# A recommender tower whose loops are unrolled, with an eighth table looked up by matmul and its feature store transposed

## The reference, cut to what matters

```python
e = jnp.stack([tbl_0[ids[:, 0]], ..., tbl_25[ids[:, 25]]], axis=1)      # 2048 x 26 x 128
combined = jnp.concatenate([dense[:, None, :], e], axis=1)              # 27 features of 128
interactions = jnp.einsum('bfd,bgd->bfg', combined, combined)           # a 27 x 27 gram for each sample
flat = interactions[:, triu_i, triu_j]                                  # its 351 pairs
h = jnp.concatenate([dense, flat, dense], axis=1)                       # 607 columns
h = jnp.maximum(h @ W_top1 + b_top1, 0.0)                               # 512
h = jnp.maximum(h @ W_top2 + b_top2, 0.0)                               # 256
y = h @ W_top3                                                          # 2048 x 1
```

## Time and profile before

| | value |
|---|---|
| timed executions, median | 425.34 us |
| span of the profiled execution | 696.8 us |
| mean granted clock of TensorE in it | 0.740 |
| PE, DVE, ACT, POOL busy in it | 54%, 30%, 13%, 45% |
| share of the ending chain put down to "issue" | 29% |
| share put down to "another core or an unknown queue" | 16% |

### The profile page before, as it was taken

The page is one execution under the profiler, slowest core; times in us unless marked ns, Lnnn a source line. Parts: engine busy times, 40 slices in busy tenths (PEclk is TensorE's granted clock), DMA queues, the critical chain, the costliest instruction groups (busy, mean ns, idle before and its releaser), DMA issues.

```text
span 696.8 us, 13458 instructions
## 1 busy us (share of the span) xinstructions
PE 377.1 (54%) x5828; PEld 317.6 (46%) x5828; DVE 209.2 (30%) x561; ACT 92.9 (13%) x159; POOL 312.2 (45%) x308
## 2 busy tenths in 40 slices
PE   1306523396284843927349082771817547194897
PEld 1306422394174732717238071561716545083875
DVE  3524007140083100921029010461006600075121
ACT  1111000021011200202002020100201011011132
POOL 6770546304537054470736617174271733637100
PEclk9757755598588775977769595695858858588798
DMA  5651111111101111030101201012010200101000
GB/s 163 189 159 61 41 38 47 31 54 37 41 15 53 64 42 34 21 104 4 49 26 29 100 12 53 16 38 87 20 53 8 98 26 27 49 7 52 19 3 2
DMA packets 18087, 34.32 MB, mean 49 GB/s; under 512 B 8241, under 2 KB 10929, under 8 KB 18065
## 3 DMA queue, kind: packets, MB, share of 16 engines
q0 software_dynamic: 9728, 19.94, 10.0%
q1 hardware_dynamic: 8338, 14.06, 6.1%
HBM read 33.97 MB, written 0.01 MB: 49 GB/s over the span
## 4 chain that ended last, share of the span: by engine, by line
PE 47%; issue 29%; another core or an unknown queue 16%; DMA 4%; ACT 3%; DVE 1%; SPq 0%; ACTq 0%
PE flip_ps L306 15%; PE gram_ps L323 12%; PE flip_ps L290 6%; PE mlp_ps L348 6%; PE mlp_ps L357 5%; DMA raw_then_y<-tbl 4%; ACT feats L456 2%; PE mlp_ps L350 2%; PE mlp_ps L376 1%; ACT hi L619 1%; PE pairs_ps L336 0%; ACT xT L546 0%; ACT xT L549 0%; DVE dots L468 0%
## 5 line engine op out<-in xcount | busy, mean ns | idle before, releaser
L269 POOL DMA_INDIRECT emb<-tbl,idx x304 | 312.0, 1026 | 336.4 <-DMA idx<-ids 225.5
L306 PE MATMUL flip_ps<-marks,hi 125*128 125x256 f32 x448 | 129.6, 321 | 106.0 <-ACT feats L456 102.0
L323 PE MATMUL gram_ps<-feats 128*27 128x27 f32 x4096 | 86.2, 202 | 169.2 <-issue 165.6
L448 DVE COPY feats<-flip_ps 128x512 f32<-128x512 f32 x56 | 38.5, 688 | 400.8 <-remote 247.9
L323 PEld LDWEIGHTS gram_ps<-feats 128*27 128x27 f32 x4096 | 63.7, 113 | 200.1 <-issue 198.6
L306 PEld LDWEIGHTS flip_ps<-marks,hi 125*128 125x128 f32 x448 | 98.8, 220 | 110.9 <-issue 69.7
L484 DVE TENSOR_SCALAR marks<-id_cols,row_no 125x256 fp32r<-125x256 int32 x448 | 127.5, 362 | 32.8 <-remote 25.1
L306 PE MATMUL flip_ps<-marks,lo 125*128 125x256 f32 x448 | 124.6, 310 | 0.9 <-issue 0.9
L306 PEld LDWEIGHTS flip_ps<-marks,lo 125*128 125x128 f32 x448 | 98.7, 220 | 2.1 <-issue 1.8
L290 PE MATMUL flip_ps<-ident,emb 128*128 128x128 f32 x320 | 62.2, 320 | 31.2 <-issue 18.2
L456 ACT COPY feats<-flip_ps 128x512 f32<-128x512 f32 (+1 forms) x32 | 31.5, 984 | 237.0 <-remote 126.1
(11 more groups left out here) (23 smaller groups left out, 77.9 us busy)
## 6 DMA issues: line engine op xcount, KB each, us to landing
id_cols<-ids_in_pairs SPq DMA_DIRECT2D x8, 896.0 KB
emb<-tbl,idx POOLq DMA_INDIRECT x304
emb<-dense SPq DMA_DIRECT2D x16, 64.0 KB
raw_then_y<-tbl SPq DMA_DIRECT2D x2, 500.0 KB
dots<-tbl SPq DMA_DIRECT2D x2, 500.0 KB
h1T<-tbl SPq DMA_DIRECT2D x2, 500.0 KB
w1p_sb<-w_pairs SPq DMA_DIRECT2D x1, 702.0 KB
w_sb<-w SPq DMA_DIRECT2D x1, 512.0 KB
```

What stands on the lines that cost most here:

```text
L269: nc.gpsimd.indirect_dma_start(emb[:, u, f, :], None, tables[order[f - 1]][:, :], bass.IndirectOffsetOnAxis(ap=idx[:, u, order[f - 1]:orde ...
L306: last = nc.tensor.matmul(flip_ps[:, m % 2, 2 * (s % 2):2 * (s % 2) + 2, :], part[s][0:R[s], c, :], marks[0:R[s], s % MARK_SLOTS, c, :], s ...
L323: last = nc.tensor.matmul(gram_ps[QUAD * j:QUAD * j + F, n, 0:F], row, row, start=True, stop=True)
L448: copy(feats[:, u, :, GROUP * k:GROUP * k + n], flip_ps[:, m % 2, 0:n, :].rearrange("d f p -> d p f")).then_inc(s_kept[m % 2], 1)
```

## The change

The batch is now cut so that a tile is 128 neighbouring samples. All loops are written out. Eight tables are looked up by matmul (the eighth has 1,250 rows, 10 for a partition) and 18 gathered, 288 gathers in all. `emb` has three slots; the third is also a staging place of raw tables, so its first gathers wait until all tables of pair 0 were looked up. All ids are loaded at the start, and the dense features come already transposed (`dense_sb`), so that they are neither loaded by tile nor flipped. The small tables come repacked into one array with 128 partitions (rows past 125 are zero), and there are five staging places. `feats` is `[d, u, feature, sample]`, so that the 27 operands of a gram lie 128 floats apart. Marks are made and used by half tables, with four half-table slots. There are three flip banks, and ACT alone copies out of them. On PE the look-ups of a pair stand together, ahead of a "weave" of gram and flips of the next tile; the rest of the layers of the pair before comes between the two weaves of a pair.

```diff
-LOOKED_UP = 7
-GATHERED = F - LOOKED_UP
+LOOKED_UP = 8
+GATHERED = TABLES - LOOKED_UP
+SLOTS = 3
+FLIP_BANKS = 3
...
-        emb = sb("emb", [P, 2, GATHERED, P])
+        emb = sb("emb", [P, SLOTS, GATHERED * P])
-        marks = sb("marks", [P, MARK_SLOTS, MAX_CHUNKS, 2 * P], fp32r)
+        marks = sb("marks", [P, MARK_SLOTS, HALF_CHUNKS, 2 * P], fp32r)
-        feats = sb("feats", [P, 2, P, FEAT_PITCH])
+        feats = sb("feats", [P, 2, F, P])
...
+            def load_table(s):
+                sp.dma_start(waiting(s), small_rows[:, FIRST_CHUNK[s]:FIRST_CHUNK[s] + N_CHUNKS[s], :]
+                             ).then_inc(s_raw[s % PLACES], 16)
...
+            sp.dma_start(idx[:, 0, :], ids_by_sample[:, 0, :]).then_inc(s_idx[0], 16)
+            load_table(0)
             load_columns(0)
...
-            body(0, True)
-            with pool.Fori(1, pairs) as i:
-                body(i, False)
+            for t in range(tiles):
+                v = t % SLOTS
+                if t < 2:
+                    pool.wait_ge(s_idx[t], 16)
+                if t == SLOTS - 1:
+                    pool.wait_ge(s_looked, 2 * LOOKED_UP)
+                if t >= SLOTS:
+                    pool.wait_ge(s_flip, GROUPS * (t - SLOTS + 1))
+                for k in range(GROUPS):
+                    for f in features_in(k):
+                        nc.gpsimd.indirect_dma_start(
...
-                        row = feats[:, u, QUAD * j + n, 0:F]
+                        row = feats[:, u, 0:F, QUAD * j + n]
...
+            def looking_up(i):
+                for k in range(LOOK_GROUPS):
+                    look_up(i, k)
+                    if i and k == 1:
+                        pair_rows(2 * i - 1)
+            def weave(t):
+                for part in range(4):
+                    gram(t, part)
+                    flip(t + 1, part)
+                flip(t + 1, GROUPS - 1)
+            def layers(i):
+                first_layer(i - 1, BOTH, 2 * (i - 1), range(1, 3))
+                pair_rows(2 * i)
+                first_layer(i - 1, BOTH, 2 * (i - 1), range(3, H1C))
                 second_layer(i - 1, BOTH)
                 third_layer(i - 1, BOTH)
...
+            looking_up(0)
+            for k in range(GROUPS):
+                flip(0, k)
+            weave(0)
+            pair_rows(0)
+            weave(1)
+            for i in range(1, pairs):
+                looking_up(i)
+                first_layer(i - 1, BOTH, 2 * (i - 1), range(0, 1))
+                if i < last:
+                    weave(2 * i)
+                    layers(i)
+                    weave(2 * i + 1)
+            for part in range(4):
+                gram(2 * last, part)
+            layers(last)
+            first_layer(*LAST[0], 2 * last)
+            second_layer(*LAST[0])
+            third_layer(*LAST[0])
+            for k in range(GROUPS):
+                flip(2 * last + 1, k)
+            for part in range(4):
+                gram(2 * last + 1, part)
+            pair_rows(tiles - 1)
+            first_layer(*LAST[1], tiles - 1)
...
+            for s in range(LOOKED_UP):
+                act.wait_ge(s_raw[s % PLACES], 16 * (s // PLACES + 1))
+                nc.scalar.copy(hi[s][0:R[s], :, :], waiting(s)[0:R[s], :, :]).then_inc(s_hi, 1)
+                if s % 2 and s > 2:
+                    keep_looked(0, s // 2 - 1)
```

More of the change, by code:

```diff
@@ L73, in tower @@
     order = feature_order([t.shape[0] for t in tables])
-    small = [tables[t] for t in order[GATHERED - 1:]]
+    small = [tables[t] for t in order[GATHERED:]]
     R = [row_chunk(t.shape[0]) for t in small]
@@ L77, in tower @@
     MAX_CHUNKS = max(N_CHUNKS)
-    dense_v = dense.rearrange("(p t) d -> p t d", t=tiles)
-    ids_v = ids.rearrange("(p t) f -> p t f", t=tiles)
-    out_v = out.rearrange("(p t) o -> o p t", t=tiles)
+    FIRST_CHUNK = [sum(N_CHUNKS[:s]) for s in range(LOOKED_UP)]
+    HALF_CHUNKS = -(-MAX_CHUNKS // 2)
+    assert LOOK_GROUPS == 4 and H1C == 4 and H2C == 2 and GROUPS == 5
     ctx = ExitStack()
@@ L278, in _, with await_bank @@
         @block.tensor
         def _(pe):
[L280 to L288 removed]
+            def await_bank(m):
+                if m >= FLIP_BANKS:
+                    pe.wait_ge(*emptied_by[m - FLIP_BANKS])
@@ L312, in gram @@
-            def gram(i, u, rows, first):
-                if rows[0] == 0:
-                    for bank in range(2):
-                        pe.wait_ge(s_kept[bank], kept_before(i, (FLIP[1][0], PER_PAIR)[u], bank))
-                    if not first or u:
-                        pe.wait_ge(s_blocks, 2 * (2 * i + u))
-                for n in rows:
-                    for j in range(P // QUAD):
-                        row = feats[:, u, QUAD * j + n, 0:F]
+                    for x in range(2):
+                        h = 2 * s + x
+                        pe.wait_ge(s_marked, 2 * LOOKED_UP * i + h + 1)
+                        for c in range(half):
+                            for part in (hi, lo):
+                                last = nc.tensor.matmul(
+                                    flip_ps[:, m % FLIP_BANKS, 2 * (s % 2):2 * (s % 2) + 2, :],
+                                    part[s][0:R[s], half * x + c, :],
+                                    marks[0:R[s], h % MARK_SLOTS, c, :],
+                                    start=(x == 0 and c == 0 and part is hi),
+                                    stop=(x == 1 and c == half - 1 and part is lo))
+                        last.then_inc(s_looked, 1)
@@ L451, in keep_looked @@
-        def keep_looked(engine, copy, i, k):
-            m, f, n = LOOK[k], GATHERED + 2 * k, len(looked_in(k))
-            engine.wait_ge(s_looked, LOOKED_UP * i + 2 * k + n)
-            copy(feats[:, :, :, f:f + n].rearrange("d u p f -> d f u p"),
-                 flip_ps[:, m % 2, 0:2 * n, :].rearrange("d (f u) p -> d f u p", u=2)).then_inc(s_kept[m % 2], 1)
+            last = pairs - 1
+            for i in range(1, pairs):
+                looking_up(i)
[4 more added lines that the diff above has]
+                    weave(2 * i + 1)
@@ L628 @@
+            activate(*LAST[0], FIRST_LAYER)
+            activate(*LAST[0], SECOND_LAYER)
+            keep_y(*LAST[0], pairs - 1)
+            for k in range(GROUPS):
+                keep(tiles - 1, k)
+            keep_pairs(tiles - 1)
+            activate(*LAST[1], FIRST_LAYER)
+            activate(*LAST[1], SECOND_LAYER)
+            keep_y(*LAST[1], pairs - 1)
 def kernel(**inputs):
```

511 lines of the change are left out of this document (223 added, 288 removed).

## The result

The changed kernel takes **439.7 us** (437.2 to 442.0, four runs) against 425.4 for the kernel before beside it: a ratio of 1.0354, interval 1.0296 to 1.0411. The forecast was 406 us, with a range of 392 to 426. A second comparison gave 439.0 against 424.2, 1.0357.

The account below looks back on a forecast made before the run. POOL's gathers were taken to bound the kernel; fewer gathers gave 20 us, eaten by two tiles' serial PE work at the end, leaving the head's 18.7: 405.9 against 425.3, forecast 406 us, range 392 to 426.

Parts of the forecast that it names:

- What bounds the kernel before: POOL paces the timed run, 47.4 us a pair against PE's 36.8; most profiled idle time belongs to that profile alone.
- Point 1: One table fewer for POOL to gather: 288 gathers, the last ending at 364.9 us, saving 17.5 on later tiles.
- Point 2: Head, look-ups of pair 0: DVE done near 44 us, last products near 47, so tile 2 doesn't wait.
- D: Rival at the head: tables don't come faster and tile 2 waits 10 us, 416 us in all; chance 0.11.
- Point 3: Third `emb` slot, ids and dense features preloaded: earns nothing, as POOL's waits after the head are zero.
- Point 5: Scattered gram operands on PE from transposed `feats`: taken at nothing, with 6.9 us a gram as upper bound.
- Rival B: PE's scattered reads cost g extra a gram; hidden by POOL up to 2.7, 470 us at 6.9; chance 0.14.
- Point 4: PE needs 39.5 us a pair against POOL's 44.9; ACT takes over DVE's copies, ten at 0.59 a pair.
- longer streams with the loops written out: Written-out loops: costed at nothing, covered by the 5.4 us a pair between PE's work and POOL's.
- Point 6: After T, the end of tile 14's gathers (342.4), serial PE work ends the span at T + 63.5, 405.9 us.
- C: Rival: PE already paces the timed kernel before, so fewer gathers earn nothing; 420 us; chance 0.12.
- PE never idles: Sign on PE: together with POOL's gathers 1.25 us apart, it would mean the pace was PE's.

Follow-up runs that it names:

- b0_before: The kernel before itself, unchanged, profiled again in a job of the usual kind: 423.69 us against 424.22, ratio 0.9984.
- b2_18: The kernel before with one gather of each tile left out: 407.91 us, ratio 0.9616.
- b3_head: The kernel before with two of ACT's copies of pair 0's looked-up groups placed between its roundings: 418.42 us, ratio 0.9872.
- the first job: Four kernels timed together with the kernel before on chip 0, where the kernel before took 682.6 us instead of 424.
- k1_rows_b: Changed kernel with `feats` back in [sample, feature] rows, gram operands packed: 416.20 us, 0.9818; as k1_rows in the first job, 0.9586.
- b1_columns_b: The kernel before with `feats` stored by feature, then sample: 485.8 us, four runs from 475.6 to 487.8.
- k3_moving: Changed kernel with the gram's stationary operand packed and only the moving one scattered: 412.4 us beside 424.2 before.
- k7_rows_order: Changed kernel with old `feats` rows, look-ups between even tiles' flips, odd grams whole, last tile's flips between layers: 408.41 us, 0.963.
- k9_order: Changed kernel, new `feats` layout kept, with the PE order of k7_rows_order: 425.07 us, ratio 1.0022.

## Why the prediction was wrong, step by step

**What bounds the kernel before: right.** b0_before, b2_18 and b3_head bear out the pace of POOL at 1.248 us, the single wait at the 39th gather and the end. Reading the pace from POOL rather than from a chain with 45% of "issue" and "unknown" was right. What was too strong is that the idle time "belongs to the profiled execution alone": the first job shows timed runs of that kind.

**Point 1, gathers: right.** Where the gram reads packed rows, the last gather ends at 363.6 (364.9).

**Point 2, the head: right.** DVE's marks of pair 0 end at 39.0 (44), and the last looked-up copy is this row of ACT's timeline, changed kernel:

```profile
40.34 0.58 ACT L499 COPY feats<-flip_ps 128x512 f32<-128x512 f32 x1 [6.91 <-PE flip_ps L282]
```

The core moved 280 GB/s over the first 40 us (the first row of the stretches above) where the earlier trace rows has 159, so D is out. With the rule of the Trainium skill cited there (5 engines for 125 partitions, 16 for 128) the trace agrees: 107 GB/s for the tables before, some 230 now for all loads (tables, id columns, weights) beside the gathers' 52, with the DMA engines busy for 0.79 instead of 0.44. The 373 as the rate of the tables is not borne out.

**Point 3** claimed nothing, and POOL never waits for a slot by more than 0.3 us. The slot hides PE's lateness from POOL, though: in the changed kernel tile 14's last gather ends at 355.0 (354.06 + 0.94 in POOL's timeline above), and its flips are done only at 369.6 (368.70 + 0.87 in PE's). That lag shows only after the last gather.

**Point 5, scattered gram operands at nothing: this is the step that failed.** The reason given was that a record lasts 0.2 us while the next follows after 10 ns, so its reads would be under way beside others. The runs show that 64 products take 1.56 us from start to start instead of 0.77 (0.55 where packed ones run undisturbed), and that the layout alone is worth 22.8 us. The bounds held it: a gram takes 6.8 us in the weave, so g = 3.8, between 0 and 6.9. The value should not have been the lower end: the only row on scattered access gave a price for each element, and the argument against it rested on no row. Rival B was there with its formula: 406 + 2 x 3.8 + 6 x (7.6 - 5.4) = 427 us. By the Trainium skill ("Advanced Engine Details and Errata", "Memory Cachelines") accesses that each go to another 16-byte line pay, and two hits on a line are needed to absorb the latency. The trace agrees: 1.27 us for 128 products at 8 bytes, two to a line, beside 1.26 packed, and 1.97 at 16 bytes, one to a line. The rule gives no size, and that 512 bytes cost nearly three times as much as 16 (1.96 against 0.71 us) doesn't follow from it; why is open.

**Point 4, PE at 39.5 us a pair: too low by 1.3 even with grams corrected.** 39.5 + 7.6 is 47.1 and the pair takes 48.4. Put that in B's sum and the total closes: six pairs at 48.4 - 44.9 = 3.5 are 21.0, two grams of the end 7.6, 406 + 28.6 = 434.6, with the span at 435.4. By start times over the five pairs, a pair is 17.7 us of look-ups (16.5 with DVE's part), 4.9 of flips (4.0), 13.9 of grams (13.6), 11.4 of layers (10.9), 0.6 of pair transposes (0.9), and nothing of the 1.2 set aside for waits on ACT. ACT could have been such a wait, for beside scattered grams it takes up to three times as long, as here in the changed kernel (ACT's timeline):

```profile
98.82 1.56 ACT L526 ACTIVATE h1T<-mlp_ps,b_sb 128x256 f32<-128x256 f32 x1 [1.21 <-PE mlp_ps L330]
...
101.05 1.79 ACT L419 COPY feats<-flip_ps 128x512 f32<-128x512 f32 x1 [0.67 <-PE flip_ps L264]
```

The flips need those copies to empty their banks, but PE was so late itself that in these pairs it never stood for one. "ten at 0.59 a pair" was read from copies with a packed gram beside them; for the copies of 512 columns it became 1.41 on average, 1.78 at the median. Gathers lengthen too, 16.5 us above 0.944 each, summed, against 1.4 in k1_rows_b. PE was the slower one all the same (48.4 against 47.2 us a pair), so that cost little here. In b1_columns_b, where POOL paces, it cost the most.

**Point 4 again, "longer streams with the loops written out: I cost them at nothing": also wrong, by about 8 us.** It is hidden in the changed kernel, whose scattered products are slow enough (0.3 us of "issue" in its gram group above, 7.7 in the kernel before), and appears as soon as they are packed. In k1_rows_b tile 14's gram and the last one take 7.5 and 7.0 us instead of 3.0 each, with a stop of 1.4 to 2.8 us after each 128 products. The step to the next 128 hardly depends on how long the products themselves take: from 394.96 to 398.97 in k1_rows_b and from 391.79 to 395.80 in k3_moving it is 4.01 us, so slower products only shorten the stop. That is 8.5 of the 9.0 us by which its end was longer than point 6 said. The cover named, POOL's 5.4 us a pair, was real but isn't there behind the last gather. That the stops belong to written-out code is borne out by b0_before: of its six, four lie in the written-out pairs 0 and 7 and two in the first pass of the loop, at 113 and 126 us, and the other five passes have none. What PE waits for in them the profile doesn't name.

**Point 6, the end:** the sequence was right. With grams of 7 us, T + 63.5 becomes T + 72, and k1_rows_b shows T = 341.2 and an end at 413.6, T + 72.4. That this serial work was a choice and not a need was not seen: in another order it is 5.5 us (k7_rows_order beside k1_rows_b) to 15.5 us shorter (k9_order beside the changed kernel).

**C** falls: k1_rows_b has more PE work than the kernel before and is faster. Of the signs of being wrong, "a 37th gather after 55 us" and "POOL waiting on flips" did not occur; "grams of 6 us and more" did. The sign of PE as the pace, "PE never idles", came with gathers not 1.25 but 1.31 us apart.

Left open: why a job is of one kind or the other, by what path PE's reads slow ACT, DVE and the gathers, and why 512 bytes cost more than 16. The changed kernel itself was not run in a job of the slow kind.

## What to carry to other kernels

When a layout is turned to please the engine that writes it, count the reads: here each value is written once and read twice, as moving operand and as weights, and ACT's gain of 0.5 us a copy cost PE 3.8 us a gram. Where no row shows an access pattern and a rule and the nearest row both speak against it, take a value inside the bounds and compute at which size the pace changes engine. A median over stretches with stops isn't the pace of the products in them: compare runs without a stop. Work that is hidden under a pacing engine comes back, at its full price, behind that engine's last instruction.

## What the runs showed of the hardware

- 128 of TensorE's fp32 gram products (four column bands in turn) take 1.26 us with packed operands, 1.27 with elements 8 bytes apart, 1.97 at 16 and 3.22 at 512 bytes; with one operand packed and the other at 512 bytes 2.17 (moving) and 2.18 (weights).
- With both operands at 512 bytes such reads slow others that use SBUF: ACT copies from 0.59 to 1.78 us (median), runs of 32 DVE marks from 8.5 to 14.5 us, single gathers from 0.94 to 12.7 us (b1_columns_b). With one operand packed ACT's copies stay at 0.62.
- Small products written out one after another stop for 1.4 to 2.8 us after each 128, with their 128 weight loads (k1_rows_b); the next 128 come after 4.01 us whether the products take 1.26 or 2.17 us. In a loop the stops are gone after the first pass (b0_before).
- In one job, and in one profiled execution besides, the same kernel takes 682 to 697 instead of 424 us, PE standing before gram products for 110 to 166 us with nothing to wait for (k1_rows, and the first profile of the kernel before).
